# A fused MoE / gated-recurrence / MoE kernel: the sixth projection of the following block placed in front of the output products, and filler matmuls taken out

## The reference, cut to what matters

```python
z = layernorm(x)
q, k, v, g = z @ Wq, z @ Wk, z @ Wv, z @ Wg
a = z @ Wa                        # 512 wide: real and imaginary half
a = sigmoid(abs(a)) * exp(1j * angle(a))
h = associative_scan(a1*a2, a2*x1 + x2) over (a, k * v)   # along the sequence
y = real((q * h * silu(g)) @ Wo)
y = layernorm(y + z) * ln1_scale + ln1_bias
out = gelu(y @ W1 + b1) @ W2 + b2
x = x + layernorm(out + y) * ln2_scale + ln2_bias
```

## Time and profile before

| | |
|---|---|
| median of 3 runs | 700.74 us (699.93 to 701.62) |
| profiled execution, its own time | 700.4 us |
| its span (first to last instruction) | 698.7 us |
| mean granted PE clock, share of full | 0.979 |
| PE, DVE, ACT, POOL busy | 94%, 68%, 64%, 28% |

### The profile page before, as it was taken

The page is one execution under the profiler, slowest core; times in us unless marked ns, Lnnn a source line. Parts: engine busy times, 40 slices in busy tenths (PEclk is TensorE's granted clock), DMA queues, the critical chain, the costliest instruction groups (busy, mean ns, idle before and its releaser), DMA issues. The chain is left out here.

```text
span 698.7 us, 12032 instructions
## 1 busy us (share of the span) xinstructions
PE 658.3 (94%) x4568; PEld 573.5 (82%) x4568; DVE 476.2 (68%) x1040; ACT 450.4 (64%) x812; POOL 195.3 (28%) x290
## 2 busy tenths in 40 slices
PE   9789999999999999999999999999998999889993
PEld 8468999565688898898898898898886898589993
DVE  6834400456979989989989989988999777510001
ACT  5234443179699899798899798897796243144440
POOL 6250111220033216216216226214233221500112
PEclk9999999999899999999999999999999999989997
DMA  9989960511011011022022022011011094207700
GB/s 270 335 283 311 375 214 23 179 61 60 31 61 68 9 46 61 16 76 72 6 76 76 1 76 76 1 46 46 1 46 46 24 377 158 69 8 249 256 24 25
DMA packets 53010, 74.10 MB, mean 106 GB/s; under 512 B 4774, under 2 KB 44795, under 8 KB 52952
## 3 DMA queue, kind: packets, MB, share of 16 engines
q1 hardware_dynamic: 48600, 59.84, 26.2%
...
## 5 line engine op out<-in xcount | busy, mean ns | idle before, releaser
L1649 PE MATMUL bank<-zt_h,w_in_h 128*128 128x512 f32 x192 | 78.7, 410 | 4.7 <-DVE qg L1323 2.6
L992 PE MATMUL bank<-xdt,ring 128*128 128x160 f32 x512 | 74.9, 304 | 3.2 <-issue 1.9
L1649 PE MATMUL bank<-yt_h,w_h 128*128 128x256 f32 x256 | 73.6, 287 | 4.1 <-ACT ht_h L1630 2.3
L992 PEld LDWEIGHTS bank<-xdt,ring 128*128 128x128 f32 x512 | 71.9, 194 | 4.9 <-issue 3.6
L1651 PE MATMUL bank<-zt_h,w_in_l 128*128 128x512 f32 x192 | 75.2, 392 | 0.0
L1650 PE MATMUL bank<-zt_l,w_in_h 128*128 128x512 f32 x192 | 75.2, 392 | 0.0
L784 DVE SCALAR_TENSOR_TENSOR xo<-bank,gate,xg 128x256 f32<-128x256 f32 x20 | 9.2, 481 | 96.2 <-PE bank L1019 96.2
L1005 PE MATMUL bank<-hid,ring 128*128 128x160 f32 x512 | 72.8, 300 | 1.4 <-DVE idx_s L768 0.7
L1649 PE MATMUL bank<-w_h,ht_h 128*128 128x256 f32 x256 | 73.6, 288 | 0.0
L1005 PEld LDWEIGHTS bank<-hid,ring 128*128 128x128 f32 x512 | 70.4, 190 | 2.3 <-issue 2.3
L822 ACT ACTIVATE hid<-bank,b1t 128x160 f32<-128x160 f32 x128 | 49.9, 393 | 34.3 <-PE bank L992 10.5
...
## 6 DMA issues: line engine op xcount, KB each, us to landing
...
```

The source lines that it names most:

```text
L992: ins = T.matmul(bank[b][:, 0:CAP], w1_of(s)[:, k, m * P:(m + 1) * P], xdt[:, k, e * CAP:(e + 1) * CAP], start=k == 0, stop=k == KD - 1)
L1649: T.matmul(out, left[0], right[0], start=start, stop=False)
```

## The change

Three edits. First, in `STEPS` and in the three like periods of `LAST_STEPS`, `project 5` of the next block goes in front of `wo 0`. Second, in the same places `read 4` and `fold 4` of the next block go in front of `gated 0`. Third, the fillers in front of `wo 0` (blocks 1 to 6: 3 + 5 x 5 = 28 matmuls) and those in front of `up 0` of block 7 (4 matmuls) are gone. The rest of the lists is the same apart from line breaks. `read 4` belongs to ACT, which has no part in `gated`, so ACT's queue keeps its order.

```diff
 STEPS = (
...
-    (0, "project", 4), (-2, "up", 7), (-1, "gated", 0), (0, "read", 4), (0, "fold", 4), (-1, "gated", 1),
-    (-2, "gelu", 6), (-2, "logits", 0), (-1, "wo", 0), (0, "project", 5), (-2, "split", 6), (-2, "down", 1),
+    (0, "project", 4), (-2, "up", 7), (0, "read", 4), (0, "fold", 4), (-1, "gated", 0), (-1, "gated", 1),
+    (-2, "gelu", 6), (-2, "logits", 0), (0, "project", 5), (-1, "wo", 0), (-2, "split", 6), (-2, "down", 1),
...
 LAST_STEPS = (
...
-    (-3, "project", 4), (-5, "up", 7), (-4, "gated", 0), (-3, "read", 4), (-3, "fold", 4), (-4, "gated", 1),
-    (-5, "gelu", 6), (-5, "logits", 0), (-4, "wo", 0), (-3, "project", 5), (-5, "split", 6), (-5, "down", 1),
+    (-3, "project", 4), (-5, "up", 7), (-3, "read", 4), (-3, "fold", 4), (-4, "gated", 0), (-4, "gated", 1),
+    (-5, "gelu", 6), (-5, "logits", 0), (-3, "project", 5), (-4, "wo", 0), (-5, "split", 6), (-5, "down", 1),
...
             def wo(b, q):
...
                 wait(pe, o_attn_read, quarter_no)
-                if 0 < b.n < NB - 1 and q == 0:
-                    keep_busy(3 if b.n == 1 else 5, o_attn)
                 pe.wait_ge(yg_done, b.n * 2 + 2)
...
             def up(b, j):
...
-                if b.n == NB - 1 and j == 0:
-                    pe.wait_ge(gelu_done[0], b.n * 4)
-                    keep_busy(4, upb[0])
                 if m == 0:
                     pe.wait_ge(yt_ready, KD * (b.n * 2 + q + 1))
```

More of the change, by code:

```diff
@@ L92 @@
 STEPS = (
-    (-2, "up", 5), (-1, "turned_back", 0), (1, "z_norm", 0), (0, "fold", 2), (0, "load_quarter", 0),
-    (-1, "scan", 0), (0, "project", 3), (-1, "scan", 1), (-2, "gelu", 4), (-2, "gelu", 5), (-2, "split", 4),
-    (-1, "rotate", 0), (-2, "next_turn", 0), (0, "read", 3), (-1, "back", 0), (-2, "split", 5), (-2, "up", 6),
-    (0, "project", 4), (-2, "up", 7), (-1, "gated", 0), (0, "read", 4), (0, "fold", 4), (-1, "gated", 1),
-    (-2, "gelu", 6), (-2, "logits", 0), (-1, "wo", 0), (0, "project", 5), (-2, "split", 6), (-2, "down", 1),
@@ L98 @@
[L98 to L107, removed]
+    (-2, "up", 5), (-1, "turned_back", 0), (1, "z_norm", 0), (0, "fold", 2), (0, "load_quarter", 0), (-1, "scan", 0),
@@ new lines @@
+    (0, "project", 3), (-1, "scan", 1), (-2, "gelu", 4), (-2, "gelu", 5), (-2, "split", 4), (-1, "rotate", 0),
+    (-2, "next_turn", 0), (0, "read", 3), (-1, "back", 0), (-2, "split", 5), (-2, "up", 6), (0, "project", 4),
+    (-2, "up", 7), (0, "read", 4), (0, "fold", 4), (-1, "gated", 0), (-1, "gated", 1), (-2, "gelu", 6),
+    (-2, "logits", 0), (0, "project", 5), (-1, "wo", 0), (-2, "split", 6), (-2, "down", 1), (-2, "gelu", 7),
+    (-2, "split", 7), (-1, "mix_stats", 0), (0, "square", 0), (0, "read", 5), (0, "size", 0), (0, "root", 0),
@@ new lines @@
+    (0, "denominator", 0), (-1, "mix_norm", 0), (0, "inverse", 0), (0, "fold", 5), (-1, "mix_turn", 0),
+    (0, "load_quarter", 1), (1, "z_turn", 0), (-2, "out_stats", 1), (-1, "wo", 1), (-1, "mix_split", 0),
+    (-1, "up", 0), (-1, "up", 1), (-2, "out_norm", 1), (1, "z_low", 0), (1, "project", 0), (0, "tangent", 0),
+    (0, "gate_half", 0), (0, "gate", 0), (-1, "gelu", 0), (-1, "gelu", 1), (-1, "split", 0), (-1, "split", 1),
+    (1, "read", 0), (-1, "up", 2), (-1, "up", 3), (0, "tangent", 1), (-1, "gelu", 2), (-1, "split", 2),
@@ L108 @@
+    (-1, "gelu", 3), (2, "z_stats", 0), (-1, "split", 3), (1, "project", 1), (-1, "mix_stats", 1), (0, "phase", 0),
+    (1, "read", 1), (0, "rounding", 0), (-2, "next_turn", 1), (-1, "down", 0), (1, "fold", 1), (-1, "mix_norm", 1),
+    (-1, "mix_turn", 1), (0, "turns", 0), (-1, "out_stats", 0), (-1, "mix_split", 1), (-2, "logits", 1),
+    (3, "load_z", 0), (1, "project", 2), (1, "read", 2), (-1, "out_norm", 0), (-1, "up", 4),
 )
@@ L122 @@
     (-4, "split", 1), (-2, "read", 0), (-4, "up", 2), (-4, "up", 3), (-3, "tangent", 1), (-4, "gelu", 2),
[L123 to L155, removed]
+    (-4, "split", 2), (-4, "gelu", 3), (-1, "z_stats", 0), (-4, "split", 3), (-2, "project", 1), (-4, "mix_stats", 1),
@@ new lines @@
+    (-3, "phase", 0), (-2, "read", 1), (-3, "rounding", 0), (-5, "next_turn", 1), (-4, "down", 0), (-2, "fold", 1),
+    (-4, "mix_norm", 1), (-4, "mix_turn", 1), (-3, "turns", 0), (-4, "out_stats", 0), (-4, "mix_split", 1),
+    (-5, "logits", 1), (-2, "project", 2), (-2, "read", 2), (-4, "out_norm", 0), (-4, "up", 4), (-4, "up", 5),
+    (-3, "turned_back", 0), (-1, "z_norm", 0), (-2, "fold", 2), (-2, "load_quarter", 0), (-3, "scan", 0),
+    (-2, "project", 3), (-3, "scan", 1), (-4, "gelu", 4), (-4, "gelu", 5), (-4, "split", 4), (-3, "rotate", 0),
@@ new lines @@
+    (-4, "next_turn", 0), (-2, "read", 3), (-3, "back", 0), (-4, "split", 5), (-4, "up", 6), (-2, "project", 4),
+    (-4, "up", 7), (-2, "read", 4), (-2, "fold", 4), (-3, "gated", 0), (-3, "gated", 1), (-4, "gelu", 6),
+    (-4, "logits", 0), (-2, "project", 5), (-3, "wo", 0), (-4, "split", 6), (-4, "down", 1), (-4, "gelu", 7),
+    (-4, "split", 7), (-3, "mix_stats", 0), (-2, "square", 0), (-2, "read", 5), (-2, "size", 0), (-2, "root", 0),
+    (-2, "denominator", 0), (-3, "mix_norm", 0), (-2, "inverse", 0), (-2, "fold", 5), (-3, "mix_turn", 0),
@@ new lines @@
+    (-2, "load_quarter", 1), (-1, "z_turn", 0), (-4, "out_stats", 1), (-3, "wo", 1), (-3, "mix_split", 0),
+    (-3, "up", 0), (-3, "up", 1), (-4, "out_norm", 1), (-1, "z_low", 0), (-1, "project", 0), (-2, "tangent", 0),
+    (-2, "gate_half", 0), (-2, "gate", 0), (-3, "gelu", 0), (-3, "gelu", 1), (-3, "split", 0), (-3, "split", 1),
+    (-1, "read", 0), (-3, "up", 2), (-3, "up", 3), (-2, "tangent", 1), (-3, "gelu", 2), (-3, "split", 2),
+    (-3, "gelu", 3), (-3, "split", 3), (-1, "project", 1), (-3, "mix_stats", 1), (-2, "phase", 0), (-1, "read", 1),
@@ new lines @@
+    (-2, "rounding", 0), (-4, "next_turn", 1), (-3, "down", 0), (-1, "fold", 1), (-3, "mix_norm", 1),
+    (-3, "mix_turn", 1), (-2, "turns", 0), (-3, "out_stats", 0), (-3, "mix_split", 1), (-4, "logits", 1),
+    (-1, "project", 2), (-1, "read", 2), (-3, "out_norm", 0), (-3, "up", 4), (-3, "up", 5), (-2, "turned_back", 0),
+    (-1, "fold", 2), (-1, "load_quarter", 0), (-2, "scan", 0), (-1, "project", 3), (-2, "scan", 1), (-3, "gelu", 4),
+    (-3, "gelu", 5), (-3, "split", 4), (-2, "rotate", 0), (-3, "next_turn", 0), (-1, "read", 3), (-2, "back", 0),
@@ new lines @@
+    (-3, "split", 5), (-3, "up", 6), (-1, "project", 4), (-3, "up", 7), (-1, "read", 4), (-1, "fold", 4),
+    (-2, "gated", 0), (-2, "gated", 1), (-3, "gelu", 6), (-3, "logits", 0), (-1, "project", 5), (-2, "wo", 0),
+    (-3, "split", 6), (-3, "down", 1), (-3, "gelu", 7), (-3, "split", 7), (-2, "mix_stats", 0), (-1, "square", 0),
+    (-1, "read", 5), (-1, "size", 0), (-1, "root", 0), (-1, "denominator", 0), (-2, "mix_norm", 0),
+    (-1, "inverse", 0), (-1, "fold", 5), (-2, "mix_turn", 0), (-1, "load_quarter", 1), (-3, "out_stats", 1),
@@ new lines @@
+    (-2, "wo", 1), (-2, "mix_split", 0), (-2, "up", 0), (-2, "up", 1), (-3, "out_norm", 1), (-1, "tangent", 0),
+    (-1, "gate_half", 0), (-1, "gate", 0), (-2, "gelu", 0), (-2, "gelu", 1), (-2, "split", 0), (-2, "split", 1),
+    (-2, "up", 2), (-2, "up", 3), (-1, "tangent", 1), (-2, "gelu", 2), (-2, "split", 2), (-2, "gelu", 3),
+    (-2, "split", 3), (-2, "mix_stats", 1), (-1, "phase", 0), (-1, "rounding", 0), (-3, "next_turn", 1),
+    (-2, "down", 0), (-2, "mix_norm", 1), (-1, "busy", 6), (-2, "mix_turn", 1), (-1, "turns", 0),
@@ L156 @@
+    (-2, "out_stats", 0), (-2, "mix_split", 1), (-3, "logits", 1), (-2, "out_norm", 0), (-1, "busy", 4),
+    (-2, "up", 4), (-2, "up", 5), (-1, "turned_back", 0), (-1, "scan", 0), (-1, "scan", 1), (-2, "gelu", 4),
     (-2, "gelu", 5), (-2, "split", 4), (-1, "rotate", 0), (-2, "next_turn", 0), (-1, "back", 0), (-2, "split", 5),
     (-2, "up", 6), (-2, "up", 7), (-1, "gated", 0), (-1, "gated", 1), (-2, "gelu", 6), (-2, "logits", 0),
-    (-1, "busy", 27), (-1, "wo", 0), (-2, "split", 6), (-2, "down", 1), (-2, "gelu", 7), (-2, "split", 7), (-1, "mix_stats", 0),
@@ L159 @@
[L159 to L162, removed]
-    (-2, "next_turn", 1), (-1, "down", 0), (-1, "mix_norm", 1), (-1, "mix_turn", 1), (-1, "out_stats", 0),
@@ L164 @@
[L164 to L168, removed]
@@ L169 @@
-    (-1, "list_rows", 0),
+    (-1, "busy", 27), (-1, "wo", 0), (-2, "split", 6), (-2, "down", 1), (-2, "gelu", 7), (-2, "split", 7),
+    (-1, "mix_stats", 0), (-1, "choose", 0), (-1, "mix_norm", 0), (-1, "mix_turn", 0), (-2, "out_stats", 1),
+    (-1, "wo", 1), (-1, "mix_split", 0), (-1, "up", 0), (-1, "up", 1), (-2, "out_norm", 1), (-1, "gelu", 0),
+    (-1, "gelu", 1), (-1, "split", 0), (-1, "split", 1), (-1, "up", 2), (-1, "up", 3), (-1, "gelu", 2),
+    (-1, "split", 2), (-1, "gelu", 3), (-1, "split", 3), (-1, "count", 0), (-1, "mix_stats", 1), (-1, "place", 0),
@@ new lines @@
+    (-2, "next_turn", 1), (-1, "down", 0), (-1, "mix_norm", 1), (-1, "mix_turn", 1), (-1, "out_stats", 0),
```

(5 more changed lines are left out.)

## The result

The changed kernel takes 708.5 us (median of 4 runs, 707.5 to 712.1) against 701.2 us for the kernel before beside it (699.9 to 703.8). The ratio is 1.010, 95% interval 1.0073 to 1.0128, so it is slower by 7 us, 5 to 9. The profiled execution took 708.5 us, its span is 706.8 us (698.7 before).

What follows compares the result with a forecast made beforehand. PE, busy 94%, bounds it, with DVE's chain from the products to `yt_l` nearly as long. Block delays 1.27 + 0.63 + 1.20 + 0.63 + 1.20 + 0.85 = 5.8 us on 700.4 gave 706.2 us, range 700.5 to 710.0.

Steps and rivals of the forecast that it cites:

- the sum: Delays passed on in blocks 1 to 6 add up to 5.8 us, giving 706.2 us; own range 704.5 to 708.
- Project 5 in the hole: Ahead of the output products: project 5 takes 2.77 us without waiting, so products start 0.99 to 1.66 us later.
- The delay of `up 0`: Later products delay DVE's and ACT's chain to `yt_l`; after 0.78 us slack, `up 0` comes 0.2 to 0.9 us later.
- A second late operand: Before split 1: ACT's late `ht_h` makes DVE 0.63 to 1.30 us late, passed on to PE's second `mix_turn`.
- A price inside the chain: DVE's line 1341 takes 1.81 instead of 0.68 us when meeting POOL's addition on `xr`; expected to meet again.
- rival (b): DVE and POOL no longer meet at line 1341: 6.8 us off the chain, 699.4 us, nothing measurable; chance 0.08.
- The clock: PE's idle before `up 0` and second `mix_turn` lowers its clock: up to 3.4 us a stretch, 708 to 711; chance 0.10.
- The fillers of block 7: Ahead of `up 0` of block 7: fillers end just when the operand is there, so removing them gives 0.0.
- PE idle before `up 0`: Before `up 0`, PE is ready early and stands about 2.0 us until `yt_l` releases it.
- Rival (a): Between products and `up 0`, PE's order alone decides: the 8.8 us are kept, 691.6 us; chance 0.14.
- Rival (c): An overlooked slack after `up 0` takes up the late split: only 3.1 us lost, 703.5 us; chance 0.12.

Runs made afterwards that it cites:

- fold_only: Kernel before with only `read 4` and `fold 4` moved ahead of the gated values, fillers and project 5 staying: ratio 1.0047 to the kernel before.
- after_split: Changed kernel with split 1 put behind tangent 1 of the next block on DVE: ratio 1.0101 to the kernel before.
- after_pool: Changed kernel with POOL's addition on `xr` waiting for DVE's denominator in the first quarter of blocks 1 to 6: ratio 1.0013 to the kernel before.
- after_fill6: Changed kernel with 12 filler matmuls ahead of `up 0` of block 6: ratio 1.0104 to the kernel before.

## Why the prediction was right, and where not

The time was right: 706.2 forecast, 708.5 measured beside a kernel before that ran at 701.2, so +5.8 forecast and +7.4 by the medians, 7 by the ratio. That lies inside the range that the sum gave itself (4.1 to 7.6 us over 700.4), but it is partly luck: two parts of the sum were wrong by about 0.4 us a block, in opposite directions. Step by step:

*Project 5 in the hole.* Right: no wait in it, products 2.86 us behind the logits (2.8 forecast), DVE 1.05 us idle before `vn` (1.0; in block 3 1.61, and 1.6 forecast), fold 4 covered, and by fold_only worth its 0.6 us where it isn't.

*The delay of `up 0`.* Mechanism right, size wrong. I had put its slack at 0.78 us, and it is about 0.3. The term that failed is the half microsecond from the end of `yt_h` to that of `yt_l`. I let `yt_l`'s first part start when `yt_h`'s first part was ready. But line 1433 has one wait for both parts. In the changed kernel it takes from the end of `yt_h` at 305.14 + 0.82 = 305.96 to the end of `yt_l` at 306.07 + 0.88 = 306.95: 0.99 us. So `up 0` came 0.7 us later in even blocks (0.2 forecast) and 1.3 in odd ones (0.8).

*A second late operand.* Wrong: with `up 0` itself that late, ACT's `ht_h` is just in time for split 1, and after_split shows that the wait is worth nothing. DVE doesn't stand ahead of split 1 (0.4 us forecast), and PE's second `mix_turn` waits 0.56 us in even blocks, as before, and not at all in block 3, where I had forecast 1.0 and 0.4 us. The two errors cancel by luck: I had added 0.4 us there that belong in front of `up 0`. By block, between the ends of the logits, the loss was 1.38, 0.71, 1.31, 0.72, 1.26 and 1.28 us, against 1.27, 0.63, 1.20, 0.63, 1.20 and 0.85 forecast: 6.7 against 5.8.

*A price inside the chain.* Right: line 1341's long instruction stayed at 1.8 us in all of blocks 1 to 6, so rival (b) is out, and after_pool shows its worth, 0.9 us a block.

*The clock.* One stretch, in block 6. By after_fill6 it is worth 0.3 us of block 6, or 0.5 us by the middle stretch; block 6 lost 0.4 us beyond the forecast.

*The fillers of block 7.* Nothing, as forecast: `up 0` still starts when `yt_l` is ready, after 0.65 us of wait.

*PE idle before `up 0`*: 0.66 + 1.40 = 2.06 us (2.0 forecast). The part before `z_turn` is named "issue" in the row; by the code `z_turn` waits there for fold 5, which stands behind `vn` in DVE's queue as well.

Rival (a), PE's order alone, would have needed `up 0` 11.6 us behind the products. It came 13.95 us behind them in every block from 1 to 6. Rival (c), the short sum of 3.1 us, is out as well: nothing behind `up 0` took up its delay.
